# A transformer layer on one core: bodies written out instead of looped, and the experts' down product in float16 halves

## The chip, the cores and the metric

One core of a Trainium2 chip runs the whole kernel. The metric is the device time of one execution in microseconds (us), lower is better. One measurement of the kernel before is the median of three runs. The core has a TensorE for matrix products (PE in the profile), VectorE (DVE), ScalarE (ACT), GpSimd (POOL) and SyncE (SP), which here only issues DMAs. Each engine runs its own list of instructions in order, and the engines wait for each other through semaphores.

## The reference

```python
# x is (16, 512, 128): B sequences of S tokens of width D
def attention(x, Wq, Wk, Wv, Wo, gamma, beta):      # 16 heads of 64, causal
    q, k, v = (einsum('bsd,hde->bhse', x, W) for W in (Wq, Wk, Wv))
    attn = softmax(where(causal, q @ k^T / sqrt(64), -inf))
    y = x + concat_heads(attn @ v) @ Wo
    return (y - mean(y)) * rsqrt(var(y) + 1e-3) * gamma + beta

def experts(x, gate_w, gate_up_w, down_w):          # 32 experts of width 64, top 8
    probs = softmax(x @ gate_w.T)
    comb = top-8 of probs, divided by their sum, 0 for the other experts
    for each expert e:                               # all 32 are computed for all tokens
        g, u = split(x @ gate_up_w[e].T)
        out += comb[:, e] * ((u * silu(g)) @ down_w[e].T)
    return out

x = x + attention(layernorm(x), ...)
x = x + experts(layernorm(x), ...)
```

Everything is float32, and the kernel keeps that accuracy on a float16 TensorE by splitting operands into a high and a low float16 half.

## The kernel before

**Pipeline over sequences.** Sixteen sequences pass through a software pipeline. `body(n, now)` exists once for each engine and is the list of what that engine does in step n. It works on several sequences at once: `AHEAD` (n+2, loading and its statistics), `NEXT` (n+1, layer norm, first projections, row maxima of the scores), `CUR` (n, attention), `PREV` (n-1, rest of attention's output, second norm, routing, all experts) and `OLD` (n-2, the last units of the experts and the output). Steps run from n = -2 to n = 17. The code is straight for n = -2 to 2 and for n = 14 to 17; n = 3 to 13 are eleven turns of a hardware loop (`Fori`) on each engine, with the wait values computed from the loop's register.

**The order of work** inside a body is a fixed list for each engine, written out by hand or by a planner: the calls at the end of each `body`. No engine looks ahead of its list.

**Products.** `product(...)` makes one product from halves with three float16 matmuls: high by high, high by low, low by high. It is used for q, k, v, the output projection, the router, and the experts' gate and up. All weights but the experts' down weights are split once at the start: `largest` (DVE) takes the maximum of each, a reduction on POOL, `halve` (ACT) writes the high half and `rest` (DVE) the low half.

**Experts.** The 32 experts go in 16 units of two (`EP`), each a 128x512 tile. For unit j: `gate_product` and `up_product` on PE (banks G and U), `gate_tanh` on ACT, `gate_times_tanh` and `times_up` on DVE into `su`, `weigh_unit` on POOL, which multiplies by the routing weights that `spread_weights` (SP) has spread by DMA into `a32` (a ring of 4), and `down_product` on PE, which adds into bank X. In the kernel before the down product is one float32 matmul of `wd32` by `a32`:

```python
pe.wait_ge(a32_done, (n + rel) * EP + j + 1)
mm(bank[XB][:, :], wd32[:, j, :], a32[:, j % RING, :], j == 0, j == EP - 1).then_inc(down_mm, 1)
```

The profile shows each of these as two records `bank_x<-expert_room,wd`. After the last unit `copy_out` (ACT), `turn_out` (PE), `add_experts` (DVE) and `store` (SP) finish the sequence.

**Attention.** For each of 16 heads: `scores` (PE, three pieces), `exps` (ACT), `p_high` (ACT) and `p_low` (POOL) split the exponentials, `times_v` (PE), `denominators` and `divide` (DVE), `turn_heads` (PE), `o_high` and `o_low`, `times_wo` (PE), `add_heads` (DVE). For the maxima of the next sequence: `project`, `qk_high`, `qk_low`, `max_scores` (PE), `row_maximum` (DVE), `split_maxima` (POOL), `turn_maxima` (PE), `copy_maxima` (ACT).

**The start of a body** is a chain through all engines: `times_wo(PREV, 3)`, `add_heads`, `residual_stats` (DVE), `residual_inverse` (POOL), `residual_apply` (ACT), `add_input` and `second_stats` (DVE), `second_inverse` (POOL), `second_apply` (ACT), and then `turn_h2(PREV)` on PE, which opens the experts.

Of the kernel before, what the change touches and what calls it, by code (L numbers as in the profile page):

```python
# [7 lines left out]
ALU = mybir.AluOpType  # L8
# [3 lines left out]
P = 128  # L12
# [5 lines left out]
EP = NE // 2  # L18
LN_EPS, ATTN_LN_EPS = 1e-5, 1e-3
MAX_UNIT = 2.0 ** 13  # L20
NEG = -3.0e38
# [32 lines left out]
def layer(nc, x, wq, wk, wv, wo, gamma, beta, gate, gate_up, down, ident_c, mask_c, future_c, out):  # L54
    with ExitStack() as ctx:
# [15 lines left out]
        WCOLS = [D * 8, D * 8, D * 8, D * 8, EP * 2 * P, NE]  # L71
        WQ, WK, WV, WO, WGU, WG = range(6)
# [4 lines left out]
        wd32 = sb("wd32", [P, EP, D], F32)  # L77
# [49 lines left out]
        def unsplit(w):  # L127

            if w < WO:
                return score_ops[:, :, :, :, :].rearrange("p a b c d -> p (a b c d)").bitcast(F32)[:, WAT[w]:WAT[w] + WCOLS[w]]  # L130
            if w == WO:
                return p_lo[:, :, :].rearrange("p a b -> p (a b)").bitcast(F32)[:, 0:WCOLS[w]]
            if w == WGU:
                return expert_room[:, :, :].rearrange("p a b -> p (a b)")[:, 0:WCOLS[w]]
            return logits[:, 0, :]

        comb_rows = nc.dram_tensor("comb_rows", (NE, S), F32, kind="Internal").ap()
# [52 lines left out]
        a32_done, down_mm = sem("a32_done"), sem("down_mm")  # L190
        yT_done, yT_turned = sem("yT_done"), sem("yT_turned")
# [24 lines left out]
        def _(sp):  # L216
# [11 lines left out]
            sp.dma_start(wd32[:, :, :].rearrange("p a d -> p (a d)"), down).then_inc(wd_loaded, 16)  # L228
# [4 lines left out]
            def body(n, now):  # L233
# [52 lines left out]
                def spread_weights(rel, j):  # L286

                    if rel in now:
# [4 lines left out]
                        wait(sp, down_mm, p * EP + j - RING + 1)  # L293
# [13 lines left out]
                place_qk(CUR, 6)  # L307
                place_qk(CUR, 7)
# [4 lines left out]
                spread_weights(PREV, 1)  # L313
                place_qk(NEXT, 0)
                spread_weights(PREV, 2)
                spread_weights(PREV, 3)
                spread_weights(PREV, 4)
                load_xb(CUR)
                spread_weights(PREV, 5)
                place_qk(NEXT, 1)  # L320
                place_max(NEXT, 0)
                spread_weights(PREV, 6)
# [3 lines left out]
                spread_weights(PREV, 9)  # L326
                place_qk(NEXT, 3)
                place_qk(NEXT, 4)
                place_max(NEXT, 1)
                spread_weights(PREV, 10)  # L330
                load_x(AHEAD)
                place_qk(NEXT, 5)
                spread_weights(PREV, 11)
                place_max(NEXT, 2)
                spread_weights(PREV, 12)
                spread_weights(PREV, 13)
                spread_weights(PREV, 14)
                spread_weights(PREV, 15)
# [3 lines left out]
            for n in range(-AHEAD, 1 - OLD):  # L342
                body(n, pieces(n))
            with sp.Fori(1 - OLD, B - AHEAD) as i:
# [6 lines left out]
        def _(pe):  # L351
# [19 lines left out]
            def body(n, now):  # L371
# [169 lines left out]
                def down_product(rel, j):  # L541

                    if rel in now:
                        if j == 0:
                            take(XB, yT_done, 1, rel, 0)
                            if first(n + rel):
                                pe.wait_ge(wd_loaded, 16)
                        pe.wait_ge(a32_done, (n + rel) * EP + j + 1)
                        mm(bank[XB][:, :], wd32[:, j, :], a32[:, j % RING, :], j == 0, j == EP - 1).then_inc(down_mm, 1)
# [18 lines left out]
                project(CUR, 15, R1)  # L568
                scores(CUR, 2, 0)
                scores(CUR, 2, 1)  # L570
                times_v(CUR, 0)
                scores(CUR, 2, 2)
                max_scores(CUR, 7, 0, R0, R1)
                scores(CUR, 3, 0)
                scores(CUR, 3, 1)
                max_scores(CUR, 7, 1, R0, R1)
                turn_h2(PREV)
                times_v(CUR, 1)
                max_scores(CUR, 7, 2, R0, R1)
                scores(CUR, 3, 2)  # L580
                logit_product(PREV)
                scores(CUR, 4, 0)
                scores(CUR, 4, 1)
                gate_product(PREV, 0)
                turn_maxima(CUR, 3)
                values(CUR, 4, R0)
                scores(CUR, 4, 2)
                turn_heads(CUR, 0)
                up_product(PREV, 0)
                values(CUR, 5, R1)  # L590
                scores(CUR, 5, 0)
                times_v(CUR, 2)
                scores(CUR, 5, 1)
                turn_weights(PREV)
                times_v(CUR, 3)
                values(CUR, 6, R0)
                scores(CUR, 5, 2)
                turn_heads(CUR, 1)
                scores(CUR, 6, 0)
                scores(CUR, 6, 1)  # L600
                values(CUR, 7, R1)
                times_wo(CUR, 0)
                gate_product(PREV, 1)
                scores(CUR, 6, 2)
                turn_h(NEXT)
                scores(CUR, 7, 0)
                up_product(PREV, 1)
                gate_product(PREV, 2)
# [3 lines left out]
                up_product(PREV, 2)  # L612
                scores(CUR, 7, 1)
                gate_product(PREV, 3)
                max_scores(NEXT, 0, 0, R0, R1)
                scores(CUR, 7, 2)
                times_v(CUR, 5)
                down_product(PREV, 0)
                max_scores(NEXT, 0, 1, R0, R1)
                scores(CUR, 8, 0)  # L620
                up_product(PREV, 3)
# [1010 lines left out]
```

## Time and profile before

| | |
|---|---|
| median of three runs | 2055.48 us (2052.27 to 2055.97) |
| the profiled execution | 2053.28 us, of which its span is 2051.4 us |
| mean granted TensorE clock | 0.956 of full speed |
| PE busy | 1819.8 us (89% of the span) |
| DVE busy | 1507.4 us (73%) |
| ACT busy | 1334.3 us (65%) |
| POOL busy | 1150.6 us (56%) |
| instructions in the span | 55121 |
| DMA | 187.77 MB, 34.8% of the 16 DMA engines |

The span runs from the first to the last instruction, and the time of the execution has 1.9 us more around it. Busy is the time in which an engine has an instruction at work; a busy PE can be at the lower of its two clock levels.

### The profile page before, as it was taken

The page shows a single profiled execution, that of the slowest core. Times are in us where ns is not written, and L with a number is a line of the kernel's source. Part 1 is how long each engine was busy: PE and PEld are TensorE (multiplying, and loading weights), DVE is VectorE, ACT ScalarE, POOL GpSimd, SP SyncE. Part 2 cuts the span into 40 slices and gives each one's busy share as a digit, 9 for nine tenths or more (in the row PEclk, how much of TensorE's full clock was granted, in tenths as well). Part 3 has the DMA queues.
Part 4 walks back from the last instruction along what each step waited for, and adds up shares of the span by engine and source line. Part 5 has one row for each costly group of instructions (what it writes and reads, how often), then busy time and mean ns, then how long its engine had stood idle before and what let it go on. Part 6 is the DMA issues. An engine that isn't in the chain of part 4 may idle for free.

```text
span 2051.4 us, 55121 instructions
## 1 busy us (share of the span) xinstructions
PE 1819.8 (89%) x17728; PEld 1057.6 (52%) x17728; DVE 1507.4 (73%) x4445; ACT 1334.3 (65%) x2135; POOL 1150.6 (56%) x939
## 2 busy tenths in 40 slices
PE   2478899999999898998989899898999989999977
PEld 0145555555555555555555555555555555555642
DVE  6756787878778686877868677686867868787654
ACT  1376767677576666758666576766757666776742
POOL 3044556666556565655656565555655656655753
PEclk9699999999999999999999999999999989999999
DMA  4323242533334252342424334252333424333212
GB/s 144 72 68 84 64 120 70 135 79 105 100 90 115 55 135 74 105 105 70 120 64 122 81 97 123 55 135 60 104 101 86 118 56 125 84 105 99 75 42 89
DMA packets 180692, 191.45 MB, mean 93 GB/s; under 512 B 22464, under 2 KB 146240, under 8 KB 180160
## 3 DMA queue, kind: packets, MB, share of 16 engines
q1 hardware_dynamic: 180416, 187.77, 34.8%
q8 instruction: 174, 2.85, 0.6%
q14 instruction: 102, 0.84, 0.1%
HBM read 81.25 MB, written 5.24 MB: 42 GB/s over the span
## 4 chain that ended last, share of the span: by engine, by line
PE 78%; issue 7%; ACT 5%; DVE 2%; POOL 2%; DMA 0%; POOLq 0%; DVEq 0%; ACTq 0%; SPq 0%
PE bank_v L353 16%; PE bank_r L353 15%; PE bank_s L353 14%; PE bank_x L353 12%; PE bank_g L353 8%; PE bank_u L353 8%; PE bank_v L364 3%; ACT y L758 2%; ACT p L830 1%; ACT p_hi L750 1%; PE bank_v L435 1%; DVE max_junk L1127 1%; POOL rstd L1465 1%; PE bank_x L364 1%; POOL p_lo L1507 0%
## 5 line engine op out<-in xcount | busy, mean ns | idle before, releaser
L1507 POOL TENSOR_TENSOR p_lo<-p,p_hi 128x1280 f16<-128x1280 f32 x256 | 670.4, 2619 | 291.8 <-ACT p_hi L750 289.9
L830 ACT ACTIVATE p<-bank_s,back 128x512 f32<-128x512 f32 (+1 forms) x768 | 458.5, 612 | 110.7 <-PE bank_s L353 106.7
L1127 DVE CUSTOM_DVE_ANT_0 max_junk<-bank_r,mask 128x256 f16<-128x256 f32 (+3 forms) x920 | 407.7, 488 | 159.3 <-PE bank_r L353 121.1
L1531 POOL TENSOR_TENSOR expert_room<-expert_room 128x512 f32<-128x512 f32 x256 | 324.4, 1273 | 210.5 <-DVE expert_room L1256 163.9
L353 PE MATMUL bank_s<-score_ops 128*128 128x512 f16 (+3 forms) x2048 | 419.1, 307 | 24.2 <-ACT p L830 23.3
L750 ACT ACTIVATE p_hi<-p 128x1280 f16<-128x1280 f32 x256 | 324.9, 1269 | 37.0 <-PE bank_v L353 33.8
L353 PE MATMUL bank_x<-expert_room,wd 128*128 128x512 f32 x512 | 281.0, 637 | 38.9 <-issue 38.6
L353 PE MATMUL bank_v<-v_hi,p_hi 128*128 128x65 f16 x2560 | 264.9, 196 | 1.8 <-DVE oT L1151 1.2
L353 PE MATMUL bank_v<-v_lo,p_hi 128*128 128x64 f16 x2560 | 264.8, 194 | 0.0
L353 PE MATMUL bank_v<-v_hi,p_lo 128*128 128x65 f16 x2560 | 264.8, 195 | 0.0
L353 PEld LDWEIGHTS bank_s<-score_ops 128*128 128x128 f16 x2048 | 163.1, 99 | 191.0 <-issue 77.6
L353 PEld LDWEIGHTS bank_v<-v_hi,p_hi 128*128 128x128 f16 x2560 | 238.3, 99 | 26.9 <-issue 3.4
L750 ACT ACTIVATE nat<-bank_r 128x512 f16<-128x512 f32 x256 | 150.1, 595 | 145.6 <-PE bank_r L353 141.7
L353 PEld LDWEIGHTS bank_v<-v_lo,p_hi 128*128 128x128 f16 x2560 | 237.7, 100 | 11.4 <-issue 0.3
L353 PEld LDWEIGHTS bank_v<-v_hi,p_lo 128*128 128x128 f16 x2560 | 237.8, 98 | 0.0
L883 ACT ACTIVATE expert_room<-bank_g,back 128x512 f32<-128x512 f32 x256 | 175.6, 686 | 94.6 <-PE bank_g L353 89.1
L353 PE MATMUL bank_s<-future,ident_b 128*128 128x128 bf16 x1024 | 214.2, 222 | 0.0
L1083 DVE TENSOR_TENSOR nat<-bank_r,nat 128x512 f16<-128x512 f32 x256 | 170.7, 685 | 52.4 <-ACT nat L750 51.2
L1248 DVE SCALAR_TENSOR_TENSOR expert_room<-expert_room,bank_g 128x512 f32<-128x512 f32 x256 | 174.1, 680 | 29.5 <-ACT expert_room L883 28.7
L353 PE MATMUL bank_r<-hT,w_hi 128*128 128x512 f16 x512 | 158.2, 392 | 36.3 <-DVE hT L1076 28.4
L1256 DVE TENSOR_TENSOR expert_room<-bank_u,expert_room 128x512 f32<-128x512 f32 x256 | 175.4, 685 | 12.7 <-PE bank_u L353 11.5
L353 PE MATMUL bank_g<-h2T,w_hi 128*128 128x512 f16 x512 | 154.4, 383 | 6.3 <-DVE expert_room L1248 6.3
(128 smaller groups left out, 3081.5 us busy)
## 6 DMA issues: line engine op xcount, KB each, us to landing
score_ops<-nat SPq DMA_DIRECT2D x768, 128.0 KB, 2.4
expert_room<-comb_rows SPq DMA_DIRECT2D x512, 128.0 KB, 2.8
xt<-in_x SPq DMA_DIRECT2D x16, 256.0 KB, 3.0
xb<-in_x SPq DMA_DIRECT2D x16, 256.0 KB, 3.2
out_y<-expert_room SPq DMA_DIRECT2D x16, 256.0 KB, 2.2
expert_room<-in_gate_up SPq DMA_DIRECT2D x1, 2048.0 KB, 10.3
score_ops<-rowmaxT SPq DMA_DIRECT2D x128, 4.0 KB
wd<-in_down SPq DMA_DIRECT2D x1, 1024.0 KB, 11.7
```

The source lines that it names most:

```text
L353: return pe.matmul(dst, lhsT, rhs, start=start, stop=stop, skip_group_check=shared)
L364: last = pe.transpose(dst[:, c * P:c * P + P], src[:, c, :], ident32[:, :])
L750: return act.activation(dst, src, ACT.Copy)
L758: act.activation(dst[:, c, :], src[:, c, :], ACT.Identity, bias=shift[:, which, c:c + 1], scale=rstd[:, which, c:c + 1]).then_inc(ln_out[w ...
L830: act.activation(p32[:, h % P_SLOTS, at:at + cols], bank[score_bank(h, u)][:, 0:cols], ACT.Exp, scale=back[:, SC_SCORE:SC_SCORE + 1]).then ...
L883: act.activation(th, bank[G][:, :], ACT.Tanh, scale=back[:, SC_HALF:SC_HALF + 1]).then_inc(th_done, 1)
L1083: dve.tensor_tensor(nat[:, q % 2, (K_LO, Q_LO)[w], :], bank[b][:, :], nat[:, q % 2, (K_HI, Q_HI)[w], :], ALU.subtract).then_inc(proj_lo, 1)
L1127: done = dve.tensor_tensor_reduce(max_junk[:, k % 2, at:at + cols], bank[b][:, at:at + cols], mask[:, S - cols:S], 1.0, NEG, ALU.add, ALU. ...
L1248: dve.scalar_tensor_tensor(su[:, j % SU_SLOTS, :], th, 1.0, bank[G][:, :], ALU.add, ALU.mult).then_inc(gth_done, 1)
L1256: dve.tensor_tensor(su[:, j % SU_SLOTS, :], bank[U][:, :], su[:, j % SU_SLOTS, :], ALU.mult).then_inc(su_done, 1)
L1507: pool.tensor_tensor(p_lo[:, slot, :], p32[:, slot, :], p_hi[:, slot, :], ALU.subtract).then_inc(p_lo_done, 1)
L1531: pool.tensor_tensor(a32[:, j % RING, :], a32[:, j % RING, :], su[:, j % SU_SLOTS, :], ALU.mult).then_inc(a32_done, 1)
```

## The change

1. **Written out.** On all five engines the three parts (straight, loop, straight) become one straight run of bodies:

```diff
-            for n in range(-AHEAD, 1 - OLD):
-                body(n, pieces(n))
-            with pe.Fori(1 - OLD, B - AHEAD) as i:
-                body(i, pieces(1 - OLD))
-            for n in range(B - AHEAD, B - OLD):
+            for n in range(-AHEAD, B - OLD):
                 body(n, pieces(n))
```

2. **Down product in halves.** The down weights become a seventh split weight `WD` (16 x 128 columns), loaded into `p32` instead of `wd32`. Each unit's activations are split by two new instructions, `unit_high` on ACT and `unit_low` on POOL, into two slots each of `a_hi` and `a_lo`. `times_up` gets a factor 2^-8, which `SC_OUT` takes back.

```diff
-                        pe.wait_ge(a32_done, (n + rel) * EP + j + 1)
-                        mm(bank[XB][:, :], wd32[:, j, :], a32[:, j % RING, :], j == 0, j == EP - 1).then_inc(down_mm, 1)
+                        pe.wait_ge(a_lo_done, (n + rel) * EP + j + 1)
+                        product(bank[XB][:, :], wh(WD, j * D, D), wl(WD, j * D, D), a_hi[:, j % 2, :], a_lo[:, j % 2, :],
+                                j == 0, j == EP - 1).then_inc(down_mm, 1)
...
+                def unit_high(rel, j):
+
+                    if rel in now:
+                        p = n + rel
+                        act.wait_ge(a32_done, p * EP + j + 1)
+                        wait(act, down_mm, p * EP + j - 1)
+                        copy(a_hi[:, j % 2, :], a32[:, j % RING, :]).then_inc(a_hi_done, 1)
...
-                        dve.tensor_tensor(su[:, j % SU_SLOTS, :], bank[U][:, :], su[:, j % SU_SLOTS, :], ALU.mult).then_inc(su_done, 1)
+                        dve.scalar_tensor_tensor(su[:, j % SU_SLOTS, :], bank[U][:, :], UNIT_SHIFT, su[:, j % SU_SLOTS, :],
+                                                 ALU.mult, ALU.mult).then_inc(su_done, 1)
...
+                def unit_low(rel, j):
+
+                    if rel in now:
+                        p = n + rel
+                        pool.wait_ge(a_hi_done, p * EP + j + 1)
+                        pool.tensor_tensor(a_lo[:, j % 2, :], a32[:, j % RING, :], a_hi[:, j % 2, :], ALU.subtract).then_inc(a_lo_done, 1)
```

3. **The ring's release.** `spread_weights` j, which fills a slot of `a32`, now waits for `unit_low` of j-4 instead of its down product:

```diff
-                        wait(sp, down_mm, p * EP + j - RING + 1)
+                        wait(sp, a_lo_done, p * EP + j - RING + 1)
```

4. **At the start.** `WD` joins `largest`, `halve` and `rest`, whose loops run over four weights instead of three, and one tiny DVE instruction folds its scale into `SC_OUT`. The first `exps` of sequence 0 waits until all low halves are written, since the raw down weights lie in `p32`.

5. **All five lists are new.** The same calls stand in another order, with 16 `unit_high` and 16 `unit_low` added. The start of the PE list, for instance:

```diff
+                max_scores(CUR, 6, 2, R0, R1)
+                turn_heads(PREV, 7)
                 down_product(OLD, 12)
+                project(CUR, 14, R0)
+                down_product(OLD, 13)
                 times_wo(PREV, 3)
-                down_product(OLD, 13)
-                max_scores(CUR, 6, 2, R0, R1)
                 down_product(OLD, 14)
                 down_product(OLD, 15)
-                scores(CUR, 1, 0)
-                project(CUR, 14, R0)
-                turn_out(OLD)
+                project(CUR, 15, R1)
                 scores(CUR, 1, 1)
                 scores(CUR, 1, 2)
-                project(CUR, 15, R1)
+                turn_out(OLD)
+                max_scores(CUR, 7, 0, R0, R1)
```

`turn_h2(PREV)` comes after `scores(CUR, 3, 2)` instead of before `times_v(CUR, 1)`. On ACT `input_apply(NEXT)` moves from the start of the body to after `gate_tanh(PREV, 1)`, and `exps(CUR, 0, 0)` from the end of the body before to the start. On POOL two `unit_low(OLD)` and `add_beta(PREV)`, which stood in the middle as `add_beta(CUR)`, come ahead of `residual_inverse(PREV)`, and the rest of the list reads so:

```diff
+                weigh_unit(PREV, 0)
+                weigh_unit(PREV, 1)
+                unit_low(PREV, 0)
                 p_low(CUR, 6)
+                weigh_unit(PREV, 2)
+                unit_low(PREV, 1)
+                unit_low(PREV, 2)
...
+                weigh_unit(PREV, 14)
+                unit_low(PREV, 13)
+                weigh_unit(PREV, 15)
```

On SP `place_qk` of pair 6 moves to the end of the body before, and `spread_weights(15)` to the start of the next one.

## Rows read from the trace of the kernel before

**Rows 1.** The page: the span, and busy us with share and instructions of PE.
```profile
span 2051.4 us, 55121 instructions
PE 1819.8 (89%) x17728; PEld 1057.6 (52%) x17728; DVE 1507.4 (73%) x4445; ACT 1334.3 (65%) x2135; POOL 1150.6 (56%) x939
```

**Rows 2.** Busy time by body: stretch, its us, each engine's busy us, granted clock, DMA.
```profile
321.70:436.16 114.46, 109.40 (x1109) 64.34 (x1109) 91.89 (x276) 82.67 (x133) 70.78 (x59) 1.00 0.39 101
436.16:557.77 121.61, 112.77 (x1109) 66.26 (x1109) 91.97 (x277) 82.67 (x133) 71.35 (x59) 0.97 0.37 96
...
1532.99:1656.21 123.22, 114.51 (x1110) 67.28 (x1109) 91.36 (x275) 82.67 (x133) 70.97 (x58) 0.94 0.36 94
1656.21:1773.10 116.89, 111.73 (x1110) 65.55 (x1109) 91.05 (x275) 82.67 (x133) 70.49 (x58) 0.97 0.38 99
1773.10:1889.03 115.93, 110.82 (x1109) 64.98 (x1109) 91.40 (x270) 82.84 (x133) 69.38 (x55) 0.99 0.37 98
1889.03:1981.00 91.97, 86.70 (x961) 55.52 (x962) 55.45 (x139) 66.02 (x103) 65.76 (x44) 0.98 0.20 62
1981.00:2051.40 70.40, 47.59 (x173) 18.02 (x170) 31.61 (x73) 16.98 (x29) 24.86 (x25) 0.88 0.21 68
```

**Rows 3.** PE's waits from 430 to 1780 us: total, times, longest.
```profile
PE bank_x L353 <- issue: 38.6, 10, 4.2
PE bank_x L364 <- ACT y L758: 30.9, 11, 3.0
```

**Rows 4.** PE's timeline at one jump back of the loop: start us, us.
```profile
1283.35 2.07 PE L353 MATMUL bank_x<-expert_room,wd 128*128 128x512 f32 x2 [3.70 <-issue]
```

**Rows 5.** Busy time in ten us of body n = 2, columns as in rows 2.
```profile
340.00:350.00 10.00, 10.00 (x123) 6.81 (x122) 8.06 (x23) 9.36 (x18) 5.24 (x2) 1.00 0.13 37
```

**Rows 6.** The page: the queues that load instructions, packets, MB, share.
```profile
q8 instruction: 174, 2.85, 0.6%
q14 instruction: 102, 0.84, 0.1%
```

**Rows 7.** The chain that ended last, inside body n = 2: start us, us.
```profile
354.50 1.29 PE bank_r L353 x6
...
371.26 0.91 PE bank_x L353 x2
...
401.15 1.06 PE bank_x L353 x2
```

**Rows 8.** Groups of body n = 2: busy us, mean ns of one, idle before.
```profile
L1507 POOL TENSOR_TENSOR p_lo<-p,p_hi 128x1280 f16<-128x1280 f32 x16 | 41.9, 2619 | 16.9 <-ACT p_hi L750 16.9
...
L1531 POOL TENSOR_TENSOR expert_room<-expert_room 128x512 f32<-128x512 f32 x17 | 21.6, 1274 | 11.6 <-DVE expert_room L1256 9.3 <-DMA expert_room<-comb_rows 2.3
L750 ACT ACTIVATE p_hi<-p 128x1280 f16<-128x1280 f32 x16 | 20.3, 1269 | 2.4 <-PE bank_v L353 2.2
...
L750 ACT ACTIVATE nat<-bank_r 128x512 f16<-128x512 f32 x16 | 9.5, 596 | 7.3 <-PE bank_r L353 6.9
```

**Rows 9.** Timelines of POOL and DVE at the start of body n = 2.
```profile
324.76 2.61 POOL L1507 TENSOR_TENSOR p_lo<-p,p_hi 128x1280 f16<-128x1280 f32 x1
...
326.95 0.97 DVE L1177 TENSOR_TENSOR y<-y,gam 128x512 f32<-128x512 f32 x1 [0.38 <-ACT y L758]
```

**Rows 10.** The same DVE operation in the last body, beside an idle POOL.
```profile
1987.56 0.69 DVE L1177 TENSOR_TENSOR y<-y,gam 128x512 f32<-128x512 f32 x1 [1.20 <-ACT y L758]
```

**Rows 11.** Timelines of DVE and ACT in the head: the split of a weight of 4096 columns.
```profile
51.83 4.41 DVE L1046 TENSOR_REDUCE w_absmax<-expert_room 128x1 f32<-128x4096 f32 x1
...
83.28 4.48 DVE L1062 SCALAR_TENSOR_TENSOR w_lo<-expert_room,w_scale,w_hi 128x4096 f16<-128x4096 f32 x1
...
72.94 3.70 ACT L753 ACTIVATE w_hi<-expert_room,w_scale 128x4096 f16<-128x4096 f32 x1
```

**Rows 12.** POOL's timeline in the last body: the first and the last of 16.
```profile
2007.77 1.27 POOL L1531 TENSOR_TENSOR expert_room<-expert_room 128x512 f32<-128x512 f32 x1 [15.21 <-DMA expert_room<-comb_rows]
...
2044.11 1.26 POOL L1531 TENSOR_TENSOR expert_room<-expert_room 128x512 f32<-128x512 f32 x1 [1.05 <-DVE expert_room L1256]
```

More of the change, by code:

```diff
@@ L20 @@
 MAX_UNIT = 2.0 ** 13
+UNIT_SHIFT = 2.0 ** -8
 NEG = -3.0e38
@@ L305, in store @@
                         sp.dma_start(out[rows_of(p)].rearrange("a (c p) d -> p (a c) d", p=P), yT).then_inc(out_stored, 16)
-                place_qk(CUR, 6)
-                place_qk(CUR, 7)
+                spread_weights(OLD, 15)
                 place_max(CUR, 3)
@@ L611, in body @@
                 times_v(CUR, 4)
-                up_product(PREV, 2)
-                scores(CUR, 7, 1)
                 gate_product(PREV, 3)
                 max_scores(NEXT, 0, 0, R0, R1)
+                scores(CUR, 7, 0)
+                up_product(PREV, 3)
+                max_scores(NEXT, 0, 1, R0, R1)
+                scores(CUR, 7, 1)
+                gate_product(PREV, 4)
+                down_product(PREV, 0)
+                max_scores(NEXT, 0, 2, R0, R1)
                 scores(CUR, 7, 2)
-                times_v(CUR, 5)
@@ L659, in body @@
                 project(NEXT, 6, R0)
                 project(NEXT, 7, R1)
-                up_product(PREV, 7)
+                times_wo(CUR, 1)
+                gate_product(PREV, 8)
+                max_scores(NEXT, 3, 0, R0, R1)
+                scores(CUR, 10, 2)
+                down_product(PREV, 4)
+                times_v(CUR, 8)
+                up_product(PREV, 8)
+                max_scores(NEXT, 3, 1, R0, R1)
                 scores(CUR, 11, 0)
-                times_v(CUR, 8)
-                max_scores(NEXT, 3, 0, R0, R1)
+                times_v(CUR, 9)
@@ L739, in _ @@
             pe.wait_ge(masks_set, 1)
-            for n in range(-AHEAD, 1 - OLD):
-                body(n, pieces(n))
-            with pe.Fori(1 - OLD, B - AHEAD) as i:
-                body(i, pieces(1 - OLD))
-            for n in range(B - AHEAD, B - OLD):
+            for n in range(-AHEAD, B - OLD):
                 body(n, pieces(n))
@@ L827, in exps @@
                         act.wait_ge(score_mm, (m * H + h) * UNITS + u + 1)
+                        if first(m) and h == 0 and u == 0:
+                            act.wait_ge(w_lo_done, NW)
                         if u == 0:
@@ L950, in body @@
                 qk_high(NEXT, 2, R0)
                 qk_high(NEXT, 3, R1)
-                gate_tanh(PREV, 4)
+                exps(CUR, 8, 0)
+                unit_high(PREV, 2)
+                p_high(CUR, 7)
+                o_high(CUR, 2)
+                exps(CUR, 8, 1)
+                gate_tanh(PREV, 5)
+                unit_high(PREV, 3)
                 exps(CUR, 8, 2)
-                gate_tanh(PREV, 5)
+                qk_high(NEXT, 4, R0)
+                qk_high(NEXT, 5, R1)
+                gate_tanh(PREV, 6)
@@ L967, in body @@
-                exps(CUR, 10, 1)
-                gate_tanh(PREV, 8)
                 qk_high(NEXT, 6, R0)
                 qk_high(NEXT, 7, R1)
+                unit_high(PREV, 5)
+                exps(CUR, 10, 0)
+                gate_tanh(PREV, 8)
+                unit_high(PREV, 6)
+                exps(CUR, 10, 1)
                 exps(CUR, 10, 2)
+                p_high(CUR, 10)
                 exps(CUR, 11, 0)
-                p_high(CUR, 10)
+                gate_tanh(PREV, 9)
                 exps(CUR, 11, 1)
@@ L1020, in _ @@
                 halve(w)
-            for n in range(-AHEAD, 1 - OLD):
-                body(n, pieces(n))
-            with act.Fori(1 - OLD, B - AHEAD) as i:
-                body(i, pieces(1 - OLD))
-            for n in range(B - AHEAD, B - OLD):
+            for n in range(-AHEAD, B - OLD):
                 body(n, pieces(n))
@@ L1448, in _ @@
             dve.wait_ge(masks_set, 3)
-            for n in range(-AHEAD, 1 - OLD):
-                body(n, pieces(n))
-            with dve.Fori(1 - OLD, B - AHEAD) as i:
-                body(i, pieces(1 - OLD))
-            for n in range(B - AHEAD, B - OLD):
+            for n in range(-AHEAD, B - OLD):
                 body(n, pieces(n))
@@ L1591, in _ @@
             pool.wait_ge(w_allmaxed, 2)
-            for n in range(-AHEAD, 1 - OLD):
-                body(n, pieces(n))
-            with pool.Fori(1 - OLD, B - AHEAD) as i:
-                body(i, pieces(1 - OLD))
-            for n in range(B - AHEAD, B - OLD):
+            for n in range(-AHEAD, B - OLD):
                 body(n, pieces(n))
```

481 lines of the change are left out of this document (244 added, 237 removed).

## The prediction

> **What bounds the kernel now.** First the page: PE is busy for 1819.8 of 2051.4 us, and no other engine for more than 1507.4 [rows 1]. Then the busy time by body, cut from one down product of a body to the same one of the next [rows 2]. The reader is to see three kinds of rows. The straight bodies n = 2, 13 and 14 take 114.46, 116.89 and 115.93 us, mean 115.8. The ten stretches that contain a jump back of the loop, 436.16 to 1656.21, take 1220.05 / 10 = 122.0 us each. The work is the same: 82.67 us of ACT in all of them. The last two rows are the draining of the pipeline.
>
> In n = 2, at full clock, PE is busy for 109.40 of 114.46 us and idle for 5.06. POOL has 43.7 us idle, ACT 31.8, DVE 22.6 [rows 2]. Stretches of ten us tell where PE idles: from 340 us on it is busy for 10.00 of 10.00 [rows 5], and so it is in nearly all stretches of n = 2 and n = 14 behind the first 18 us of the body. The 5 us lie in those 18 us, where PE waits for the chain that opens the body: eleven waits of `turn_h2` for `second_apply`, 30.9 us, 2.8 each [rows 3]. Behind it a microsecond of PE work taken away is a microsecond of the body.
>
> **Part 1, the loop.** PE's waits show ten of one kind that no straight body has: 38.6 us in which PE waits for nothing that the profile shows, 4.2 at most [rows 3]. Each lies at a jump back, and the first work behind it runs at the lower of the two clock levels: one down product takes 2.07 us [rows 4] where another takes 0.91 at full clock [rows 7]. So a jump costs 3.9 us of standing still, and the rest of 122.0 - 115.8 = 6.2 us is mostly the clock that comes back late: granted 0.94 and 0.97 in rows with a jump, 1.00 in n = 2 [rows 2]. Written out, the jumps are gone: 10 x 6.2 = 62 us. Bounds: 10 x (122.0 - 116.9) = 51 and 10 x (122.0 - 114.5) = 75, from the slowest and the fastest straight body. It could only come back if straight code ran out of instructions. Straight code runs already in bodies 2 and 14, all engines at once, without such a stall. The bytes don't grow either: the two instruction queues brought 2.85 + 0.84 MB [rows 6] for 55121 instructions [rows 1], 67 bytes for each, so the loop's instructions are already fetched again in every turn.
>
> The trace shows PE standing for 3.9 us at each jump and in no straight body. The Trainium skill (Runtime: NRT & Kernel Launch, Instruction fetch mechanics) has a reason: instructions are prefetched in sequence only, and a taken branch to a far target waits for its page. By that rule the whole stall goes and nothing of it moves into straight code; the sum stays as it is.
>
> **Part 2, PE's down product.** It is now one float32 product (two records); it becomes three float16 ones like any `product`. The chain inside n = 2 prices both while PE is the limit: down products take 0.91 to 1.06 us [rows 7], and two products of three matmuls take 1.29, so 0.645 each [rows 7]. The difference is 0.26 to 0.41. The higher prices stand before matmuls with 64 rows, and a product in halves would keep some of that surplus; I take 0.30. 16 units x 0.30 = 4.8 us a body (4.2 to 6.6). Fifteen bodies, n = 1 to 15, carry a sequence's units beside attention: 15 x 4.8 = 72 us (63 to 98).
>
> **Part 3, the new work on ACT and POOL.** `unit_high` is 512 columns from float32 to float16: 0.6 us, between the 596 ns of the same size out of PSUM and 1269 ns for 1280 columns [rows 8]. 16 x 0.6 = 9.6 us a body. `unit_low` is `p_low` with 512 columns in place of 1280: 2619 x 512 / 1280 = 1.05 us by columns, 1.27 if it costs what `weigh_unit` does [rows 8]; I take 1.1, 17.6 us a body. ACT goes to 92.3, POOL to 88.4, DVE stays at 91.9 (its changed multiply: the form with a scalar costs the same in `gate_times_tanh`), all against a body of some 112: 82, 79 and 82% where PE has over 93%. Behind PE's list all of this is covered; without the cover it would cost up to 27 us a body. The unit's way is longer by two steps, but the lists give it room: unit j's down product comes about two units after its `weigh_unit`. `spread_weights` is released by `unit_low`, which comes before the down product, so the ring of four isn't held longer. On SP it is the two DMAs of each unit and those of `place_qk` behind that would be late; POOL's `weigh_unit` would wait for them.
>
> At the start of the body the chain keeps its links. Less PE work lies beside it: `scores(1, 0)`, one projection and two down products move ahead of `times_wo(3)` or shrink, while `times_v(1)` and a piece of scores come in. On the other side `input_apply` leaves ACT there. On POOL `unit_low` 14 and 15 and `add_beta` now stand before `residual_inverse`; behind that wait ACT's and DVE's norms and then `turn_h2`. The idle of 5.1 us can go to nothing or double. For it, and for lists in which four engines are above 79%, I take 1.0 us more a body: 15 us, with bounds of -75 and +75.
>
> `unit_low` also reads where DVE reads. One DVE multiply with both operands in SBUF takes 0.97 us beside a running `p_lo` [rows 9] and 0.69 beside an idle POOL [rows 10]. A body has few such, at most 0.3 us each in a chain: inside the 1.0. The Trainium skill (SBUF — State Buffer, Who interferes with whom) says that a DVE instruction with two SBUF inputs is shut out by a GpSimd instruction that reads, and one with at most one isn't; the trace agrees, and by the rule too most DVE work here, which reads one operand from PSUM, is untouched. The sum by the rule is the same.
>
> **Part 4, the ends.** In the head `WD` adds 2048 columns to three steps, half of what 4096 cost: 2.2 us and 2.2 on DVE, 1.9 on ACT [rows 11]. DVE is the one that the head follows there: +5 us (2 to 8). The late wait of the first `exps` costs nothing: those instructions now stand behind that point in ACT's list. In the last body nothing covers the units. POOL's multiplies run from 2007.77 to 2044.11, 2.42 us a unit [rows 12], where POOL works 1.27. It will work 1.27 + 1.1 = 2.4 and wait for ACT in between: 2.8 a unit, 15 x 0.4 = 6, and the last unit's way is 1 longer: +7 us (0 to 20).
>
> **The sum,** against the profiled execution, 2053.3 us (2051.4 and 1.9 around it; 0.1% below the median, 2055.5): 2053.3 - 62 - 72 + 15 + 5 + 7 = 1946. A full body would then be 115.8 - 4.8 + 1.0 = 112.0 us.
>
> **The rivals.** A, the forecast: PE stays the limit, both parts pay. Its own range is 1912 to 1980, a body of 109.8 to 114.3. Chance 0.68.
>
> B, the product's gain goes into waits: the down products stand in PE's list in front of scores and maxima, and each now waits for a way over ACT and POOL. If that costs 0.3 us a unit, a body stays at 115.8 and only the loop pays: 2053.3 - 62 + 12 = 2003; range 1980 to 2040. For it: three engines above 79%, ACT already at 9.36 of ten in one stretch [rows 5]. Against it: POOL's idle of 43.7 us and the distance in the lists. Chance 0.19.
>
> C, the new lists also close the gap at the start of the body: 15 x up to 6.4 us (5.1 of idle, 1.3 of clock), a body of 106 to 109.5, time 1855 to 1910. For it: the stall has one place and one cause. Against it: the chain has no link fewer. Chance 0.05.
>
> D, straight code stalls for instructions: 3.9 us of standing in each body, with its clock, takes the 62 us back: 2008. Against it: n = 2 and n = 14. Chance 0.03.
>
> E, slower than before: POOL becomes the limit. Its list is in order and waits alternately for `exps`, maxima, DMAs and now ACT. It has 88.4 us of work; if it keeps all of its 43.7 us of waits, a body takes 132. The change loses once each of the fifteen bodies is (62 - 12) / 15 = 3.3 us above a straight one, at 119.1, so it decides once POOL keeps over 30.7 of the 43.7. At 121 to 132 the time is 2080 to 2245. For it: nothing on POOL may pass anything. Against it: those waits are for PE's pace, and shrink as POOL grows. Chance 0.04; 0.01 is left for no change.
>
> **The numbers.** 1946 us, as A is the likeliest. The range 1912 to 1990 holds A and the near part of B, leaves out C, E and most of B and D. From the cases: faster by over 0.2% (about what a measurement can tell) 0.95, same 0.01, slower 0.04.
>
> **What would show it.** Right: no waits of 3.9 us without a cause; full bodies of 110 to 114 us; three bank X records a unit, 0.65 us in the chain; PE busy about 104.6 us a body at full clock and idle about 6, still in the first 18 us; `unit_high` 0.6, `unit_low` 1.1 us; a last body longer by some 7. Wrong: PE waiting for `unit_low` or for `exps` in the middle of bodies (B), idle below 2 us (C), waits with no cause at even distances (D), POOL above 95% (E).

## The result and the profile after

| | before | after |
|---|---|---|
| median | 2053.88 us (2048.51 to 2055.97, 4 runs) | 2004.07 us (2002.56 to 2004.57, 4 runs) |
| ratio | | 0.976, interval 0.9739 to 0.9781 |
| profiled execution, span | 2053.28, 2051.4 | 2002.56, 2000.8 |

The change makes the kernel 50 us faster. The forecast was 107 us faster, 1946, with a range to 1990: the direction was right, the size was not, and the time lies outside the range.

First the page of after, the lines that answer to [rows 1] and [rows 6], and two groups of the new work, read as [rows 8]:
```profile
span 2000.8 us, 51225 instructions
PE 1770.4 (88%) x17984; PEld 1025.5 (51%) x17984; DVE 1553.5 (78%) x4448; ACT 1469.7 (73%) x2392; POOL 1437.7 (72%) x1195
...
q8 instruction: 145, 2.38, 0.5%
q14 instruction: 110, 0.90, 0.1%
...
L1556 POOL TENSOR_TENSOR a_lo<-expert_room,a_hi 128x512 f16<-128x512 f32 x256 | 296.6, 1160 | 147.0 <-ACT a_hi L746 144.8
...
L746 ACT ACTIVATE a_hi<-expert_room 128x512 f16<-128x512 f32 x256 | 160.0, 625 | 67.2 <-PE bank_x L354 44.4
```

The new instructions cost what they were priced at: 1160 ns for `unit_low` (1.1 forecast), 625 for `unit_high` (0.6). PE is down by 49 us only. And DVE, to which the change gives nearly nothing, is up by 46 us, from 1507.4 [rows 1] to 1553.5. That is the line which points to the trouble.

Busy time by body, columns as in [rows 2], each stretch cut from the start of one `x` (the second instruction of `add_input`) to the next:
```profile
325.90:443.08 117.18, 109.10 (x1130) 63.45 (x1127) 94.64 (x276) 91.13 (x150) 88.94 (x75) 0.97 0.38 99
1140.24:1256.30 116.06, 109.36 (x1131) 63.91 (x1128) 94.76 (x277) 90.93 (x150) 88.97 (x75) 0.97 0.38 100
1720.77:1836.67 115.90, 109.22 (x1130) 63.91 (x1127) 93.71 (x268) 90.92 (x150) 88.94 (x75) 0.97 0.38 98
```

The full bodies now take 115 to 117, mean 116.1, as the straight ones of before took 115.8. But the clock is at 0.97 in nearly all of them, and DVE is busy some 3 us longer for the same work as in [rows 2]. PE's waits over the whole kernel:
```profile
PE bank_v L354 <- DVE o L1165: 36.3, 16, 2.7
...
PE bank_v L354 <- issue: 27.5, 15, 2.4
PE bank_x L365 <- ACT y L754: 19.3, 16, 9.8
```

The ten waits of 3.9 us without a cause [rows 3] are gone. Of those for `second_apply` almost nothing is left in the bodies (the longest, 9.8, is in the ends). In their place stand sixteen waits for DVE's `divide` (`o`), one per body, 2.3 us each. What was DVE doing? Its timeline at the start of one body, and POOL's beside it:
```profile
1138.80 1.40 DVE L1198 TENSOR_TENSOR y<-y,gam 128x512 f32<-128x512 f32 x1 [0.43 <-ACT y L754]
1140.24 2.99 DVE L1201 TENSOR_TENSOR x<-y,xb 128x512 f32<-128x512 f32 x1
...
1144.79 0.42 DVE L1165 TENSOR_TENSOR o<-bank_v,rden 128x256 f32<-128x256 f32 x1
...
1137.04 2.62 POOL L1525 TENSOR_TENSOR p_lo<-p,p_hi 128x1280 f16<-128x1280 f32 x1
1140.01 2.67 POOL L1525 TENSOR_TENSOR p_lo<-p,p_hi 128x1280 f16<-128x1280 f32 x1 [0.35 <-ACT p_hi L746]
```

The two instructions of `add_input` take both operands from SBUF, 0.69 us each beside an idle POOL [rows 10]. Here they take 1.40 and 2.99. The first `p_lo` ends at 1137.04 + 2.62 = 1139.66, and `y*gam` at 1140.20, 0.54 later. The second ends at 1142.68, and `x` at 1143.23, 0.55 later. Each looks like an instruction that stands until POOL's ends and then does its work. In all fifteen bodies `x` ends 0.54 to 0.56 us behind that `p_lo`. `divide`, for which PE waits, stands in DVE's list behind them.

Before, only the first of them was hit. Timelines of before, at the start of body n = 2, behind the ones of [rows 9]:
```profile
329.57 2.62 POOL L1507 TENSOR_TENSOR p_lo<-p,p_hi 128x1280 f16<-128x1280 f32 x1 [2.20 <-ACT p_hi L750]
...
327.95 0.69 DVE L1180 TENSOR_TENSOR x<-y,xb 128x512 f32<-128x512 f32 x1
```

There the second `p_lo` waited 2.20 us for ACT's `p_hi`, and `x` slipped through the gap. In the new lists it waits 0.35 and starts 0.23 us before `x`. The first hit helps the second: had `y*gam` taken 0.69, `x` would have started 0.48 us before this `p_lo` (1138.80 + 0.69 + 0.04 = 1139.53 against 1140.01). What it would have taken then, no run shows. ACT's timeline tells why the second `p_lo` comes earlier, before and then after:
```profile
325.28 1.64 ACT L758 ACTIVATE y<-y,shift,rstd 128x128 f32<-128x128 f32 x4
326.82 1.03 ACT L830 ACTIVATE p<-bank_s,back 128x512 f32<-128x512 f32 x2
327.75 0.59 ACT L750 ACTIVATE nat<-bank_r 128x512 f16<-128x512 f32 x1
328.22 1.27 ACT L750 ACTIVATE p_hi<-p 128x1280 f16<-128x1280 f32 x1
```
```profile
1135.03 0.60 ACT L746 ACTIVATE nat<-bank_r 128x512 f16<-128x512 f32 x1
1135.58 1.05 ACT L828 ACTIVATE p<-bank_s,back 128x512 f32<-128x512 f32 x2
1137.12 1.65 ACT L754 ACTIVATE y<-y,shift,rstd 128x128 f32<-128x128 f32 x4 [0.49 <-POOL shift L1485]
1138.68 1.25 ACT L746 ACTIVATE p_hi<-p 128x1280 f16<-128x1280 f32 x1
```

`exps(CUR, 1, 1)`, `exps(CUR, 1, 2)` and `qk_high(CUR, 15)` stood between `residual_apply` and `p_high` in ACT's list and now stand ahead of both. So by these timelines the new lists made the meeting, not the new instructions; no kernel with ACT's old order and the new product was run. One row for each kernel tells how general the hit on `x` is: all records of `x`, shortest, median and longest in ns, before and after.
```profile
L1180 DVE TENSOR_TENSOR x<-y,xb x16: 691/692/694, 211.6 to 1988.3; 128x512 f32<-128x512 f32 x16
```
```profile
L1201 DVE TENSOR_TENSOR x<-y,xb x16: 691/2992/2995, 210.8 to 1933.5; 128x512 f32<-128x512 f32 x16
```

The starts of `x` also cut every kernel into the same four pieces, and the forecast with them (each piece of before, with its terms of the sum):

| us | head, to the 1st `x` | 14 full bodies (each) | 15th to 16th `x` | from there to the end |
|---|---|---|---|---|
| before | 211.6 | 1683.8 (120.3) | 93.0 | 63.1 |
| forecast | 216.6 | 1568 (112.0) | 89.2 | 70.1 |
| after | 210.8 | 1625.9 (116.1) | 96.9 | 67.3 |

### The profile page after: what moved, and what is told of

Same layout as the page of the kernel before. It is cut to its first block, busy times and chain, and to the rows that moved or that the text cites. A ratio compares the mean times of both kernels' runs of the same rounds, so it can differ in the third digit from the quotient of the medians.

```text
span 2000.8 us, 51225 instructions
## 1 busy us (share of the span) xinstructions
PE 1770.4 (88%) x17984; PEld 1025.5 (51%) x17984; DVE 1553.5 (78%) x4448; ACT 1469.7 (73%) x2392; POOL 1437.7 (72%) x1195
## 4 chain that ended last, share of the span: by engine, by line
PE 65%; DVE 13%; ACT 6%; issue 5%; POOL 5%; DMA 1%; DVEq 0%; POOLq 0%; ACTq 0%; SPq 0%
PE bank_r L354 15%; PE bank_v L354 12%; PE bank_s L354 12%; PE bank_g L354 8%; PE bank_x L354 7%; PE bank_u L354 6%; PE bank_v L365 3%; DVE x L1201 2%; ACT y L754 2%; POOL rstd L1483 2%; POOL p_lo L1525 1%; DVE chosen L1243 1%; DVE stats L1051 1%; DVE max_junk L1148 1%; ACT h L754 1%
## 5 line engine op out<-in xcount | busy, mean ns | idle before, releaser
L828 ACT ACTIVATE p<-bank_s,back 128x512 f32<-128x512 f32 (+1 forms) x768 | 444.8, 610 | 80.2 <-PE bank_s L354 76.2
L354 PE MATMUL bank_s<-score_ops 128*128 128x512 f16 (+3 forms) x2048 | 406.1, 303 | 2.5 <-ACT p L828 0.9
L1556 POOL TENSOR_TENSOR a_lo<-expert_room,a_hi 128x512 f16<-128x512 f32 x256 | 296.6, 1160 | 147.0 <-ACT a_hi L746 144.8
L354 PEld LDWEIGHTS bank_s<-score_ops 128*128 128x128 f16 x2048 | 153.7, 98 | 136.5 <-issue 33.6
L746 ACT ACTIVATE a_hi<-expert_room 128x512 f16<-128x512 f32 x256 | 160.0, 625 | 67.2 <-PE bank_x L354 44.4
L1277 DVE SCALAR_TENSOR_TENSOR expert_room<-bank_u,expert_room 128x512 f32<-128x512 f32 x256 | 175.2, 684 | 6.9 <-PE bank_u L354 3.4
```

The costliest lines, as they stand in the source:

```text
L354: return pe.matmul(dst, lhsT, rhs, start=start, stop=stop, skip_group_check=shared)
L746: return act.activation(dst, src, ACT.Copy)
L828: act.activation(p32[:, h % P_SLOTS, at:at + cols], bank[score_bank(h, u)][:, 0:cols], ACT.Exp, scale=back[:, SC_SCORE:SC_SCORE + 1]).then ...
L1277: dve.scalar_tensor_tensor(su[:, j % SU_SLOTS, :], bank[U][:, :], UNIT_SHIFT, su[:, j % SU_SLOTS, :], ALU.mult, ALU.mult).then_inc(su_done, 1)
L1556: pool.tensor_tensor(a_lo[:, j % 2, :], a32[:, j % RING, :], a_hi[:, j % 2, :], ALU.subtract).then_inc(a_lo_done, 1)
```

## The experiments

Two theories after the result. **T1:** both parts pay as forecast, and the collision in `add_input` takes about 50 us back. **T2:** rival B, the product's gain is lost in waits over ACT and POOL, or it never was as large. Nine kernels tell them apart. All were compared with the kernel before on the same chip, whose medians were 2051 to 2055 us. In the expectations `u1` is kernel 1, `p1` kernel 3, and the changed kernel is the one that is called after here.

**1. The loop alone.** The kernel before with its bodies written out on all five engines, and nothing else. The edit, on each engine:
```diff
-            for n in range(-AHEAD, 1 - OLD):
-                body(n, pieces(n))
-            with pe.Fori(1 - OLD, B - AHEAD) as i:
-                body(i, pieces(1 - OLD))
-            for n in range(B - AHEAD, B - OLD):
+            for n in range(-AHEAD, B - OLD):
                 body(n, pieces(n))
```

> The kernel before with its bodies written out and nothing else changed. All theories: the ten jumps cost 6.2 us each, so 2054 - 62 = 1991 us (1979 to 2003), bodies of 115 to 117 us and no wait of 3.9 us without a cause. If so, the product in halves with its lists gave nothing or lost up to 13 us beside it (2004 against 1991). If the time stays above 2030, straight code brings stalls of its own.

Measured: 1986.93 us (1983.63 to 1989.28), ratio 0.9671 [0.9643, 0.97]. Writing out is worth 66 us, where 62 were forecast. A stretch from its middle, nearly one body long:
```profile
800.00:914.90 114.90, 110.75 (x1108) 64.97 (x1108) 92.13 (x276) 81.98 (x133) 70.15 (x59) 0.99 0.38 99
```

In the table's pieces this kernel has 214.3, 1616.7 (115.5 a body), 93.0 and 62.8. So the other part of the change, product and lists together, did not gain 45 us beside it but lost 17.

**2. The new form in the loop.** The kernel after, with the diff above reversed.

> The changed kernel with the hardware loop put back for n = 3 to 13. Loop theory: 2004 + 62 = 2066 us, so above the kernel before. Rival (the gain of 50 us came from the product in halves, and straight code gave little): 2010 to 2030.

Measured: 2102.07 (2100.83 to 2107.35), ratio 1.0234 [1.0206, 1.0262]. Slower than expected by 36 us: the new lists lose 98 us in the loop, the old ones 66. Three of PE's largest waits:
```profile
PE bank_v L358 <- POOL p_lo L1541: 28.1, 14, 2.3
...
PE bank_r L358 <- issue: 24.5, 11, 2.7
PE bank_v L369 <- issue: 23.4, 10, 2.5
```

The jump's stall is in the last two rows. It falls into two waits a turn now, 48 us in all where [rows 3] have 38.6. The first row isn't the jump's: it is `times_v(0)`, which waits in every body of after too, where the profile names no cause (27.5 us above). Here it names `p_lo`, and PE goes on 0.13 us after `p_low(0)` ends. The span is 104.6 us longer than that of after. 30 of these are PE's busy time, at a granted clock of 0.941 for 0.962, and 75 its idle time, of which the jump's two waits are 48. Why the new lists lose 98 us and the old ones 66 is not shown; that the engines behind a jump come late, and by how much depends on the lists, is a guess.

**3. The collision taken away.** `add_input` gets its first operand from PSUM: ACT's `residual_apply` writes into bank X, and both DVE instructions read it there. POOL's list and its timing are left as they are.
```diff
-                        norm_apply(n + rel, 1, y0, y0)
+                        wait(act, out_ready, n + rel)
+                        norm_apply(n + rel, 1, y0, bank[XB][:, :].rearrange("p (c d) -> p c d", c=C))
...
-                        dve.tensor_tensor(y0[:, :, :], y0[:, :, :], gam[:, :, :].to_broadcast([P, C, D]), ALU.mult).then_inc(yg_done, 1)
+                        dve.tensor_tensor(bank[XB][:, :].rearrange("p (c d) -> p c d", c=C), bank[XB][:, :].rearrange("p (c d) -> p c d", c=C), gam[:, :, :].to_broadcast([P, C, D]), ALU.mult).then_inc(yg_done, 1)
...
-                        dve.tensor_tensor(x1[:, :, :], y0[:, :, :], xb[:, :, :], ALU.add).then_inc(x1_done, 1)
+                        dve.tensor_tensor(x1[:, :, :], bank[XB][:, :].rearrange("p (c d) -> p c d", c=C), xb[:, :, :], ALU.add).then_inc(x1_done, 1)
```

> The changed kernel, but ACT writes the normed residual into bank X (free there) and DVE's two instructions of add_input read it from PSUM, so each has one operand in SBUF. Port theory (DVE with two SBUF operands stands until POOL's p_low ends, and this is on the chain that opens a body): the two take 0.7 us each instead of 1.40 and 3.00, the chain is 3.0 us shorter, a body 3 to 4.5 us (part of it clock), time 1935 to 1960 us. Rival (the chain is late for other reasons, the two long instructions are covered): within 8 us of 2004, with the two at 0.7 us all the same. Second rival (the record is long but nothing is blocked): they stay at 1.4 and 3.0.

Measured: 1953.11 (1949.09 to 1953.67), ratio 0.9504 [0.9477, 0.9532], 51 us less than after. The timeline of DVE at the start of a body, POOL's beside it, and busy time of such a body:
```profile
1113.93 0.70 DVE L1199 TENSOR_TENSOR bank_x<-bank_x,gam 128x512 f32<-128x512 f32 x1 [0.45 <-ACT bank_x L754]
1114.67 0.69 DVE L1202 TENSOR_TENSOR x<-bank_x,xb 128x512 f32<-128x512 f32 x1
...
1112.15 2.61 POOL L1526 TENSOR_TENSOR p_lo<-p,p_hi 128x1280 f16<-128x1280 f32 x1
1115.17 2.61 POOL L1526 TENSOR_TENSOR p_lo<-p,p_hi 128x1280 f16<-128x1280 f32 x1 [0.41 <-ACT p_hi L746]
```
```profile
1002.12:1114.67 112.55, 107.74 (x1124) 63.44 (x1124) 91.75 (x277) 90.75 (x150) 88.92 (x75) 0.98 0.39 103
```

`y*gam` runs in full beside a `p_lo` and takes 0.70 us in every body, so reading one operand from PSUM is enough. `x` now starts 0.50 us before its `p_lo` and lies beside it for its last 0.19 us. A body takes 112.7 us, near the 112.0 of the forecast. In the table's pieces this kernel has 212.5, 1578.2, 93.9 and 67.3. The 3.4 us a body that come back are 1.9 of PE's idle time (6.70 to 4.81 by the windows) and 1.6 of PE at the lower clock (109.36 to 107.74 busy), so a delay of 3.0 on the chain costs nearly as much again as it leaves idle.

**4. The control.** The same edit on kernel 1, where `x` is not hit anyway.

> u1_before_written_out with add_input out of PSUM as in p1. A control: in that order of work the second instruction takes 0.69 us already and the first 0.98, so at most 0.3 us a body are to be had: 1980 to 1992 us. If it gains 30 us or more here too, the gain of p1 is not that of the lost collision.

Measured: 2004.68 (2002.46 to 2006.17), ratio 0.9755 [0.9724, 0.9787]: 18 us slower than kernel 1, and outside the expected 1980 to 1992, though the edit gains nothing like the 30 us of the rival. In the old ACT list `exps` stand behind the wait for bank X, and PE's waits for both grow, by 15 us together; kernel 1 and this one:
```profile
PE bank_x L360 <- ACT y L750: 49.4, 16, 8.8
...
PE bank_s L349 <- ACT p L822: 21.4, 31, 1.6
```
```profile
PE bank_x L360 <- ACT y L750: 54.5, 16, 9.3
PE bank_s L349 <- ACT p L823: 31.7, 31, 1.6
```

The PSUM form is not faster by itself. What it brings in kernel 3 is the collision that it takes away, net of such costs, so the collision may have cost more than the 51 us.

**5. Another way round the collision: a wait.** The kernel after, plus one wait.
```diff
                 p_low(CUR, 0)
+                if PREV in now:
+                    pool.wait_ge(x1_done, n + PREV + 1)
                 p_low(CUR, 1)
```

> The changed kernel with one added wait: POOL starts p_low(CUR, 1) only when add_input has finished. Port theory: the second instruction of add_input takes 0.7 us instead of 3.0 (the first stays at 1.4), p_low(1) starts about 0.9 us later, second_inverse comes 1.3 us earlier: a body 1 to 2.5 us shorter, 1965 to 1990 us by a wait that was added. Rival (the length of the instruction has another cause): 3.0 stays and the time is 2004 to 2020.

Measured: 1974.40 (1972.17 to 1976.04), ratio 0.9614 [0.9583, 0.9645]. A wait, added and nothing taken away, makes the kernel 30 us faster. Timeline of DVE, and the record of POOL that now stands back:
```profile
1121.21 1.40 DVE L1198 TENSOR_TENSOR y<-y,gam 128x512 f32<-128x512 f32 x1 [0.43 <-ACT y L754]
1122.64 0.69 DVE L1201 TENSOR_TENSOR x<-y,xb 128x512 f32<-128x512 f32 x1
...
1123.41 2.62 POOL L1525 TENSOR_TENSOR p_lo<-p,p_hi 128x1280 f16<-128x1280 f32 x1 [1.35 <-DVE x L1201]
```

`x` is back at 0.69, `y*gam` still pays for the first `p_lo`, and PE waits 14.0 us in all for the delayed one. This kernel holds the operands, the order of the lists and the product as in after, so the cause is the overlap itself.

**6. A third way: the order.** The kernel after with `p_low(CUR, 1)` behind `second_inverse`.
```diff
                 p_low(CUR, 0)
-                p_low(CUR, 1)
                 second_inverse(PREV)
+                p_low(CUR, 1)
```

> The changed kernel with p_low(CUR, 1) moved behind second_inverse in POOL's list, so that nothing runs on POOL beside the second instruction of add_input. Port theory: that instruction takes 0.7 us instead of 3.0 (the first keeps its 1.4, since p_low(CUR, 0) stays), but p_low(1) comes some 4 us later and times_v(1) with it, so only part comes back: 1970 to 2000 us. Rival (it isn't p_low that lengthens it): it stays at 3.0 and the time rises to 2010 to 2040 by the later p_low.

Measured: 2005.27 (2001.64 to 2005.78), ratio 0.9759 [0.9731, 0.9787], nothing gained, above the expected 1970 to 2000. The tile view of `x` and PE's largest wait:
```profile
L1201 DVE TENSOR_TENSOR x<-y,xb x16: 691/693/694, 213.9 to 1936.7; 128x512 f32<-128x512 f32 x16
```
```profile
PE bank_v L354 <- POOL p_lo L1525: 61.9, 18, 4.4
```

The collision is gone here too, but `times_v(1)` waits 3.4 us a body for a `p_lo` that comes too late. In kernel 5 that `p_lo` starts 0.8 us behind the start of `x`, here 4.2 us (1148.95 and 1144.74 in one body), and the results lie 31 us apart.

**7. The product put back.** Kernel 3, with the down product again one float32 matmul. The raw weights lie in the memory of `WD`'s two halves; `unit_high` and `unit_low` still run but nothing uses what they write, and the ring of `a32` is released by the product, as before.
```diff
-                        wait(sp, a_lo_done, p * EP + j - RING + 1)
+                        wait(sp, down_mm, p * EP + j - RING + 1)
...
                         pe.wait_ge(a_lo_done, (n + rel) * EP + j + 1)
-                        product(bank[XB][:, :], wh(WD, j * D, D), wl(WD, j * D, D), a_hi[:, j % 2, :], a_lo[:, j % 2, :],
-                                j == 0, j == EP - 1).then_inc(down_mm, 1)
+                        mm(bank[XB][:, :], wd32(j), a32[:, j % RING, :], j == 0, j == EP - 1).then_inc(down_mm, 1)
```

> p1_add_input_psum with the down product back in float32 (one matmul of the raw down weights by a32, the ring released by down_mm), while unit_high, unit_low, all lists and the split's steps stay. The price that the prediction gave: 0.30 us a unit on PE, 4.8 us a body, 15 bodies: 1953 + 72 = 2025 us (2015 to 2050). Rival (PE isn't the limit any more under the new lists): 1960 to 1985.

Measured: 2051.91 (2050.03 to 2062.52), ratio 0.9998 [0.9979, 1.0017], 99 us more than kernel 3 and just above the expected range. A body takes 119.7 us against 112.7:
```profile
924.64:1044.32 119.68, 111.18 (x1130) 64.10 (x1127) 92.60 (x278) 91.33 (x150) 88.79 (x74) 1.00 0.36 97
```
```profile
PE bank_x L358 <- POOL a_lo L1565: 19.1, 16, 1.8
```

The difference is 7.0 us a body where 4.8 were forecast. Not all of it is matmul time: the last row shows a wait for `unit_low` of 1.2 us a body, of which kernel 3 has 3.2 us in all, and the ring is held longer. A kernel made for the float32 product would not have that wait, so the 7.0 isn't the price of the product alone.

**8. The low half left out.** Kernel 3 without its 256 `unit_low`; the third matmul of a down product reads the high half a second time. The low half of the experts' activations is missing from the output.
```diff
-                        pe.wait_ge(a_lo_done, (n + rel) * EP + j + 1)
-                        product(bank[XB][:, :], wh(WD, j * D, D), wl(WD, j * D, D), a_hi[:, j % 2, :], a_lo[:, j % 2, :],
+                        pe.wait_ge(a_hi_done, (n + rel) * EP + j + 1)
+                        product(bank[XB][:, :], wh(WD, j * D, D), wl(WD, j * D, D), a_hi[:, j % 2, :], a_hi[:, j % 2, :],
```

> p1_add_input_psum without the 256 unit_low: the third matmul takes a_hi in place of a_lo, so the product leaves out the low half of the activations; the ring is released by unit_high. PE's work is the same. Theory (POOL's new work is covered in full bodies and costs only in the two that drain the pipeline): 1940 to 1951 us, bodies 1 to 14 within 0.5 us of 112.7. Rival B of the prediction (the down products wait for the way over ACT and POOL): 1 us a body or more, below 1938.

Measured: 1945.93 (1943.31 to 1946.73), ratio 0.9474 [0.9445, 0.9504], 7 us less. A full body:
```profile
1000.00:1112.60 112.60, 106.70 (x1129) 62.84 (x1128) 91.82 (x278) 91.07 (x150) 71.17 (x59) 1.00 0.39 103
```

POOL has some 18 us less to do than in kernel 3 (88.92 to 71.17), and the body takes 112.6 all the same. Of the 7 us, 5.8 come from the draining: 2.1 in the body behind the fifteenth `x` and 3.8 after it. The fourteen full periods together differ by 1.5. So POOL's step isn't on PE's path in full bodies, which rejects E and POOL's half of B. ACT's half goes by the waits: PE stands 2.9 us in the whole kernel after for `unit_low`, which comes behind `unit_high`. The row also prices the product: 106.70 us of PE at a clock of 1.00 against 111.18 at 1.00 in kernel 7. That is 4.5 a body or 0.28 a unit, where the forecast said 0.30. (Neither stretch is cut exactly from `x` to `x`. Those that are, at a clock of 1.00, have 110.7 to 111.1 and 106.3 to 106.4: 4.3 to 4.7 a body.) The rest of kernel 7's 7.0 us is mostly waits.

**9. One more instruction of that kind.** Kernel 3, and `chosen` (DVE, in the routing) compares with bank X instead of the copy of it in SBUF.
```diff
-                        dve.tensor_tensor(chosen[:, :, :], dropped[:, :, :], logits[:, :, :], ALU.not_equal).then_inc(chosen_done, 1)
+                        dve.scalar_tensor_tensor(chosen[:, :, :], bank[XB][:, 0:C * NE].rearrange("p (c e) -> p c e", c=C), w_back[:, WG:WG + 1],
+                                                 dropped[:, :, :], ALU.mult, ALU.not_equal).then_inc(chosen_done, 1)
```

> p1_add_input_psum with the other long instruction of two SBUF operands mended: the comparison that writes chosen (2.0 us mean here and in u1, 0.29 for 128x128 beside an idle POOL) reads the router's product from bank X, which still holds it, in place of its copy in SBUF. Port theory: it takes 0.3 to 0.4 us. It is 1.7 us of the chain in nearly every body, but PE has attention's work beside it, so 0 to 1.7 us a body: 1929 to 1953 us, likeliest 1940. If it stays at 2.0 us, the collision isn't with an operand of that kind.

Measured: 1950.45 (1946.83 to 1951.41), ratio 0.9492 [0.9457, 0.9528], the fastest kernel with the full computation, but by its runs not clearly faster than kernel 3. Its groups on DVE, and the same one in kernel 3:
```profile
L1244 DVE SCALAR_TENSOR_TENSOR chosen<-bank_x,w_back,dropped 128x128 f32<-128x128 f32 x16 | 5.6, 351 | 0.6
...
L1254 DVE TENSOR_TENSOR exm<-ex,chosen 128x128 f32<-128x128 f32 x16 | 5.6, 353 | 12.7 <-issue 11.8 <-ACT ex L863 0.8
```
```profile
L1244 DVE TENSOR_TENSOR chosen<-dropped,logits 128x128 f32<-128x128 f32 x16 | 32.1, 2006 | 0.6
```

`chosen` gives back 26.5 us in all, and the instruction behind it stands idle for 12.7 of them. In all fifteen bodies of kernel 3 `chosen` ends 0.14 to 0.15 us behind a `p_lo`, so it is the same collision. But the fourteen full periods take 1575.8 us for 1578.2: next to nothing of it is on the path that sets the time.

## Why the prediction missed

**Part 1, the loop: right.** 62 forecast, 66 measured (kernel 1). No stall of that kind came back in straight code, and the instruction queues brought 3.28 MB after 3.69 before. The one wait without a cause in after, 1.8 us a body ahead of `times_v(0)`, isn't one for instructions: PE goes on 0.09 to 0.10 us after `p_low(0)` ends in all fifteen bodies, and kernel 2's profile names `p_lo` for it. D is out.

**Part 2, the product: right in its price.** 0.30 a unit forecast, 0.28 by the PE rows of kernels 7 and 8. Three bank X matmuls take 0.645 us in the chain of kernel 3, as two of them show:
```profile
954.43 1.29 PE bank_x L354 x6
```

PE is busy for 106.5 us a body of kernel 3 at full clock, not 104.6. Some 1.5 us of that comes with the new lists, which no part of the forecast had (kernel 7, which has the old product, is at 110.7 to 111.1 where [rows 2] have 109.4); why is open. So product and lists together, without the collision, gain 1987 - 1953 = 34 us and not 45.

**Part 3, the new work: right for ACT and POOL.** The prices hold, and in full bodies the 18 us of `unit_low` are covered (kernel 8).

**Part 3, the start of the body: the step that failed.** It said "A body has few such, at most 0.3 us each in a chain: inside the 1.0", and took 1.0 us a body. The two instructions take 0.71 and 2.30 us longer, 3.0 together, and with the clock 3.4 a body. Over the fourteen periods that is 1625.9 - 1578.2 = 47.7 us of the 57 by which the forecast missed. Two faults lie in that sentence. [Rows 9] were read as a factor, 0.97 for 0.69; but `p_lo` ended at 327.37 there and `y*gam` at 327.92, 0.55 later, the same distance as in after. Only 0.42 us of the `p_lo` were left when it came. The row allowed another reading, finish some 0.55 us behind POOL's instruction, whose price goes up to 2.62 + 0.55 - 0.69 = 2.5 us, and the sum took the one sample for the bound. The trace of before spoke against that bound as well. It has `chosen`, also with both operands in SBUF, at 1.95 to 2.20 us in fifteen bodies, beside a `p_lo`, and at 0.29 in the last; its mean is the 1944 ns of this row:
```profile
L1222 DVE TENSOR_TENSOR chosen<-dropped,logits 128x128 f32<-128x128 f32 x16 | 31.1, 1944 | 0.6
```

And the new order on ACT was costed for ACT alone; that it lets `p_high(1)` follow `residual_apply` at once, and so puts `p_lo(1)` on top of `x`, was not followed. The bounds of the term, -75 to +75, would have held it; the forecast's own range did not take them in.

The Trainium skill (SBUF — State Buffer, Who interferes with whom) says that a DVE instruction with two SBUF inputs contends with a GpSimd instruction that reads SBUF, for ports that one of them holds exclusively. The traces agree: 2.99 us beside a `p_lo`, 0.69 in kernels 3, 5 and 6. "The sum by the rule is the same" was wrong: by the rule, worked out with the duration of `p_lo` instead of one sample, such an instruction can cost 2.6 us more (an estimate; 2.30 is the most seen).

**The rest, small terms.** A body of kernel 3 is 0.7 us above 112.0: 14 x 0.7 = 10. The body of the fifteenth to sixteenth `x` was costed as a full one, but it drains and hangs on POOL: +3.9 instead of -3.8 us. The head is 0.8 us shorter, not 5 longer; but the same head takes 209.1 to 213.9 us in after and kernels 3, 5, 6, 8 and 9, so this term says little. The end grew by 4.2 instead of 7, of which kernel 8 finds 3.8 in `unit_low`. Together: -5.8 + 57.9 + 7.7 - 2.8 = 57, which is the miss.

**The rivals.** The time, 2004, is nearly B's 2003 and D's 2008, and a reader of the times alone would take one of them. Neither mechanism was there. Without the collision the forecast's kernel takes 1953, within its range. That this is only 7 us off is partly luck: the loop gave 4 us more than forecast, product and lists 11 less.

**Open:** why the new lists suffer more from the jump (kernel 2), and where the 1.5 us of PE's time come from. The wait of 1.8 us a body ahead of `times_v(0)` (27.5 us in all) reads as one for `p_low(0)`; no run moved that instruction alone.

## What to carry to other kernels

Before lists are moved, look for DVE instructions with both operands in SBUF on the chain, and for long POOL instructions beside them; price the pair by where POOL's instruction ends, not by the mean of what was seen. An engine whose busy time grows without new work is the first sign of it. A PSUM operand or one wait mends it, here 51 and 30 us. Each has a price of its own: where there was next to no collision the PSUM operand lost 18 us, and a later place in the list cost all that it saved.

## What the hardware showed

- A DVE instruction of 0.69 us can take 2.99 beside a POOL instruction of 2.67; it ended 0.54 to 0.56 us behind POOL's in all fifteen bodies. One of 128x128 takes 2.13 us at 1155.04 in after, beside a `p_lo` from 1154.40 to 1157.02, where its form with bank X takes 0.35.
- A jump back of the loop, on five engines, cost 66 / 10 = 6.6 us with one set of lists and 98 / 10 = 9.8 with the other.
